# Latent attention: four heads' weighted sums on four column groups together, and an extra product of resident weights ahead of thirteen of sixteen heads' scores

## The reference, cut to what matters

```python
query = qt_c + qt_r            # 16 heads x 256 tokens x 8
key = kt_c + kt_r
value = heads(ct_kv @ Wu_v_w + Wu_v_b)
attn = jnp.einsum('bhqd,bhkd->bhqk', query, key) / scale
attn = jax.nn.softmax(attn, axis=-1)
out = jnp.einsum('bhqk,bhkd->bhqd', attn, value)
out = out.transpose(0, 2, 1, 3).reshape(b, s, d_model)
return out @ Wo_w + Wo_b
```

## Time and profile before

| | |
|---|---|
| median of 3 runs | 2129.3 us (2128.28 to 2129.81) |
| profiled execution, first to last instruction (span) | 2134.5 us |
| latent attention, first scores to last weighted sum | about 1290 to 1788 us of the span |
| TensorE clock, mean granted over the span | 0.890 of full speed |

### The profile page before, as it was taken

One profiled execution on the slowest core, in us unless ns is written; L12 is line 12 of the kernel. 1 busy time (PEld: TensorE's weight loads), 2 busy tenths in 40 slices (PEclk: granted clock), 3 DMA queues, 4 the chain that ended last, 5 costly groups with the idle time before them and its releaser, 6 DMA issues.

```text
span 2134.5 us, 38192 instructions
## 1 busy us (share of the span) xinstructions
PE 1807.3 (85%) x10652; PEld 1360.9 (64%) x10653; DVE 1259.6 (59%) x4249; ACT 688.6 (32%) x1279; POOL 585.9 (27%) x946
## 2 busy tenths in 40 slices
PE   3759993888834599479999979999999998999998
PEld 2548991444433499468888855555555555988997
DVE  2546884666544588656656645655655652656654
ACT  0115550222200255223223214444444443223222
POOL 2653775555247366631221010000000000000000
PEclk9658996787755699789999979999999999999999
DMA  5111212000001122200000000000000000000001
GB/s 196 39 45 50 61 49 92 21 18 19 5 20 43 57 58 60 57 23 11 14 15 10 1 1 1 1 1 0 0 0 0 0 0 1 1 0 0 0 1 40
DMA packets 61674, 54.01 MB, mean 25 GB/s; under 512 B 8467, under 2 KB 54932, under 8 KB 61077
## 3 DMA queue, kind: packets, MB, share of 16 engines
q1 hardware_dynamic: 51958, 34.11, 5.2%
q0 software_dynamic: 8192, 16.79, 2.6%
q10 hardware_dynamic: 1440, 2.10, 0.3%
HBM read 31.48 MB, written 21.50 MB: 25 GB/s over the span
## 4 chain that ended last, share of the span: by engine, by line
PE 70%; issue 10%; DVE 9%; POOL 6%; DMA 2%; SPq 1%; ACT 1%; POOLq 1%; DVEq 1%; ACTq 0%
PE bk L1007 14%; PE bk L1656 10%; PE bk L582 6%; PE bk L990 5%; PE bk L992 5%; PE bk L991 5%; PE bk L1644 3%; PE bk L575 3%; PE bk L1631 2%; PE bk L1582 2%; PE bk L564 2%; PE bk L566 2%; PE bk L565 2%; DMA sb_X<-x 1%; POOL sb_xf L455 1%
## 5 line engine op out<-in xcount | busy, mean ns | idle before, releaser
L1007 PEld LDWEIGHTS bk<-sb_wd,sb_sc 128*128 128x128 f32 (+1 forms) x2688 | 332.9, 191 | 24.8 <-DVE sb_X L1106 3.6
L1007 PE MATMUL bk<-sb_wd,sb_sc 128*128 128x128 f32 (+1 forms) x2688 | 336.9, 275 | 0.9 <-issue 0.8
L1092 DVE TENSOR_TENSOR sb_sc<-sb_sb_,bk 128x512 f32<-128x512 f32 x224 | 152.2, 684 | 240.5 <-PE bk L992 190.4
L112 POOL TENSOR_TENSOR sb_ln_ve<-sb_ln_mv,sb_eps 128x2 f32<-128x2 f32 (+1 forms) x48 | 9.4, 195 | 1010.2 <-DVE sb_ln_mv L104 1010.2
L1046 ACT ACTIVATE sb_sb_<-bk 128x512 f32<-128x512 f32 x224 | 133.9, 598 | 450.8 <-PE bk L992 448.4
L1910 DVE TENSOR_REDUCE sb_sc<-bk 128x2 f32<-128x512 f32 x256 | 164.6, 687 | 156.2 <-PE bk L1631 152.1
L1656 PE MATMUL bk<-sb_sa,sb_sb_ 128*32 128x256 f32 x1024 | 247.4, 385 | 0.7 <-ACT sb_sc L1805 0.7
L1818 ACT ACTIVATE sb_sa<-bk 128x512 f32<-128x512 f32 x256 | 151.1, 597 | 182.8 <-PE bk L1644 182.8
L1106 DVE SCALAR_TENSOR_TENSOR sb_X<-bk,sb_gate,sb_X 128x128 f32 (+1 forms) x576 | 161.4, 342 | 4.2 <-PE bk L1007 1.8
L582 PE MATMUL bk<-sb_w2c,sb_sb_ 128*128 x1152 | 152.1, 275 | 0.0
L368 POOL DMA_INDIRECT xs<-sb_xn,sb_send_row x128 | 128.8, 1006 | 83.6 <-DVE sb_send_row L357 48.3
(11 more groups left out here) (279 smaller groups left out, 3418.7 us busy)
## 6 DMA issues: line engine op xcount, KB each, us to landing
sb_sc<-xs SPq DMA_DIRECT2D x144, 64.0 KB, 1.8
ys<-sb_sc SPq DMA_DIRECT2D x36, 256.0 KB, 2.3
xs<-sb_xn,sb_send_row POOLq DMA_INDIRECT x128
out<-sb_X SPq DMA_DIRECT2D x1, 2048.0 KB, 8.7
sb_sa<-w SPq DMA_DIRECT2D x1, 1792.0 KB, 13.3
sb_sc<-w SPq DMA_DIRECT2D x1, 1792.0 KB, 17.8
sb_sa<-w_gu SPq DMA_DIRECT2D x1, 1760.0 KB
xs<-sb_zeros SPq DMA_DIRECT2D x24, 64.0 KB, 17.8
```

What stands on the lines that cost most here:

```text
L1007: ins = pe.matmul(bank[:, j * P:(j + 1) * P], p.hT[0:m, c % HRING, j * P:(j + 1) * P], p.wd[0:m, q * D:(q + 1) * D], start=(c == FIRST[e] ...
L1092: dve.tensor_tensor(p.hT[0:m, c % HRING, :], p.sg[0:m, c % 2, :], p.bk[2 + c % 2][0:m, :], ALU.mult)\
```

## The change

The weighted sums of four heads are issued together: at steps 5, 9, 13 and 17 instead of one head at each of steps 2 to 17, with the key half as the outer and the head as the inner loop, so that four products in a row have four different column groups. The exponentials therefore stay longer, and their ring grows from four to eight buffers; the four new ones lie in two tensors that this stage did not use (`g2b`, `be2b`). ACT's copy of the first half moves by one head (from after head 9's exponentials to after head 10's). And ahead of the scores of every head but 5, 9 and 13, PE multiplies a resident 128 x 128 weight of the mixture by 512 of its own columns (float32r), into the bank that the scores then overwrite; nothing reads that product.

```diff
--- before.py
+++ after.py
@@ -1535,6 +1535,9 @@
 HQ = P // HR
 NHQ = NH // HQ
 NPROD = 3 * HD
+NQUAD = NH // HQ
+ERING = 8
+WARM_STEPS = [h for h in range(16) if h not in (5, 9, 13)]
 LATENT = 64
 ATT_SCALE = 1.0 / float(np.sqrt(NH + 2 * LATENT))
 SEARCH_BANKS = (1, 2, 5)
@@ -1633,12 +1636,19 @@
     ins.then_inc(p.at_s1.sem, 1)
 
 
+def at_warm_pe(pe, p, bank):
+
+    pe.matmul(bank[:], p.wgh[:, 0:P], p.wgh[:, 0:W], start=True, stop=True)
+
+
 def at_scores_pe(pe, p, b, par, h):
 
     if h % (NH // 2) == 0:
         pe.wait_ge(p.at_q2.sem, p.at_q2.at(2 * b + 2 * h // NH + 1))
     if h >= 2:
         pe.wait_ge(p.at_ex.sem, p.at_ex.at(NH * b + h - 1))
+    if h in WARM_STEPS:
+        at_warm_pe(pe, p, p.bk[3 + h % 2])
     r = head_rows(h, NPROD + 2)
     for t in range(NB2):
         ins = pe.matmul(p.bk[3 + h % 2][:, t * S:(t + 1) * S], p.at_kT[par][r, h // HQ, t * P:(t + 1) * P],
@@ -1646,15 +1656,17 @@
     ins.then_inc(p.at_s2.sem, 1)
 
 
-def at_values_pe(pe, p, b, par, a):
-
-    pe.wait_ge(p.at_ex.sem, p.at_ex.at(NH * b + a + 1))
-    if a % 8 == 0:
-        pe.wait_ge(p.at_op.sem, p.at_op.at(2 * b + a // 8))
-    o = p.bk[7][HR * (a % HQ):HR * (a % HQ + 1), (a // HQ) % 2 * S:((a // HQ) % 2 + 1) * S]
+def at_values_pe(pe, p, b, par, quad):
+
+    pe.wait_ge(p.at_ex.sem, p.at_ex.at(NH * b + HQ * (quad + 1)))
+    if quad % 2 == 0:
+        pe.wait_ge(p.at_op.sem, p.at_op.at(2 * b + quad // 2))
     for t in range(NB2):
-        ins = pe.matmul(o, p.at_v[:, par, t, a, :], p.at_e[:, a % 4, t * S:(t + 1) * S],
-                        start=(t == 0), stop=(t == NB2 - 1))
+        for r in range(HQ):
+            a = HQ * quad + r
+            o = p.bk[7][HR * r:HR * (r + 1), quad % 2 * S:(quad % 2 + 1) * S]
+            ins = pe.matmul(o, p.at_v[:, par, t, a, :], p.at_e[a % ERING][:, t * S:(t + 1) * S],
+                            start=(t == 0), stop=(t == NB2 - 1))
     ins.then_inc(p.at_av.sem, 1)
 
 
@@ -1690,8 +1702,8 @@
     for h in range(NH + LAG):
         if h < NH:
             at_scores_pe(pe, p, b, par, h)
-        if h >= LAG:
-            at_values_pe(pe, p, b, par, h - LAG)
+        if h >= HQ + LAG - 1 and (h - LAG) % HQ == HQ - 1:
+            at_values_pe(pe, p, b, par, (h - LAG) // HQ)
         if h == 1:
             pe.wait_ge(p.at_kr.sem, p.at_kr.at(b + min(ahead, 1) + 1))
             at_maxima_rows_pe(pe, p, b, 1)
@@ -1801,7 +1813,7 @@
 
 def at_heads_out_act(act, p, b, half):
 
-    act.wait_ge(p.at_av.sem, p.at_av.at(NH * b + 8 * half + 8))
+    act.wait_ge(p.at_av.sem, p.at_av.at(NQUAD * b + 2 * half + 2))
     act.activation(flat(p.at_o[:, 2 * half:2 * half + 2, :]), p.bk[7][:], ACT.Copy).then_inc(p.at_op.sem, 1)
 
 
@@ -1813,12 +1825,12 @@
 def at_act_element(act, p, b, par, behind=True, ahead=2):
     for h in range(NH):
         act.wait_ge(p.at_s2.sem, p.at_s2.at(NH * b + h + 1))
-        if h >= 4:
-            act.wait_ge(p.at_av.sem, p.at_av.at(NH * b + h - 3))
-        act.activation(p.at_e[:, h % 4, :], p.bk[3 + h % 2][:], ACT.Exp, scale=ATT_SCALE).then_inc(p.at_ex.sem, 1)
+        if h >= ERING:
+            act.wait_ge(p.at_av.sem, p.at_av.at(NQUAD * b + (h - ERING) // HQ + 1))
+        act.activation(p.at_e[h % ERING], p.bk[3 + h % 2][:], ACT.Exp, scale=ATT_SCALE).then_inc(p.at_ex.sem, 1)
         if h == 1:
             at_maxima_rows_act(act, p, b, 1)
-        if h == 7 + LAG:
+        if h == 8 + LAG:
             at_heads_out_act(act, p, b, 0)
         if ahead >= 1:
             if h == 2:
@@ -2039,7 +2051,7 @@
     "mla": dict(ln_free=B, ln_stat=2 * NT, ln_rs=2 * B, xt=B, at_xc=B, at_ctp=B, at_ct=B, at_krp=B, at_kr=B,
                 at_prp=2 * B, at_q=NS1 * B, at_hc=2 * B, at_ktp=2 * B, at_kt=2 * B, at_qtp=2 * B, at_qt=2 * B,
                 at_s1=NH * B, at_mx=NH * B, at_nm=4 * B, at_q2p=2 * B, at_q2=2 * B, at_s2=NH * B, at_ex=NH * B,
-                at_av=NH * B, at_op=2 * B, at_otp=B, at_on=4 * B, at_tp=B, at_ot=B, at_wp=B, at_x1=B, at_x=B,
+                at_av=NQUAD * B, at_op=2 * B, at_otp=B, at_on=4 * B, at_tp=B, at_ot=B, at_wp=B, at_x1=B, at_x=B,
                 at_init=5),
     "swiglu": dict(_PREP, **_COMB, gt_rows=NCH * NG, up_rows=NCH * NG, silu_d=NCH * NG, hid_d=NCH * NG, exp_d=E1 * NG,
                    exp_add=TG * E1 * NG, rtg=NG, rt3=2 * NG),
@@ -2137,7 +2149,11 @@
     at = Space(t.w1h)
     w.update(at_qT=at.take(P, NHQ, S), at_qT2=at.take(P, NHQ, S))
     at = Space(t.sa)
-    w.update(at_e=at.take(P, 4, NB2 * S), at_sk=at.take(P, 2, NB2, NH, HR))
+    heads = [at.take(P, NB2 * S) for _ in range(4)]
+    w.update(at_sk=at.take(P, 2, NB2, NH, HR))
+    for bank in (Space(t.g2b), Space(t.be2b)):
+        heads += [bank.take(P, NB2 * S) for _ in range(2)]
+    w.update(at_e=heads)
     w.update(at_sk_r=w["at_sk"].bitcast(F32R))
     at = Space(t.sb_)
     w.update(at_v=at.take(P, 2, NB2, NH, HR), at_xa=at.take(P, S), at_c=at.take(P, S), at_r=at.take(P, 2, NB2, D),
```

## The result

The change made the kernel slower: 2224.58 us median (2211.16 to 2230.06, 4 runs) against 2129.56 (2128.28 to 2130.51, 4 runs) of the kernel before, run beside it, a ratio of 1.0438 (95% interval 1.0406 to 1.047). The forecast was 2110 us, with a range of 2068 to 2152. Of the rivals the slower one, C, had the right sign and mechanism, but its time (2148) too was far from the measured one.

What follows compares the result with a forecast made beforehand. PE was taken to pace the latent attention nearly alone. Four legs gave 28.4 against 31.83 us per element, 55 us over 16; low clock took back 2.2 of 3.4 us, leaving 19 us: 2110 us, range 2068 to 2152.

Steps and rivals of the forecast that it cites:

- C: Rival for the attention stage: clock alternates, half the time low, 4.2 low stretches per element, 2148 us; chance 0.20.
- two low stretches per element: Clock term of the attention stage: 1.1 us each, so 2.2 of the 3.4 us gained per element go back.
- two places: Where the clock should fall: while PE waits for DVE's keys, and where only scores, searches and added products stand between groups.
- steps 10 to 12: Between two groups, only scores, searches and added products: one low stretch expected, 1.1 us per element.
- Steps 1 to 3: Element's start, where PE waits for DVE's keys: one low stretch expected, priced at 1.1 us.
- Leg 1: Projection to keys: DVE's twelve instructions end it, four added products fit, unchanged at 6.75 us.
- Leg 2: Keys to queries: 3.65 us at full clock, against 4.28 before.
- Leg 3: Queries to first search: 3.5 us against 4.20, with ACT's copies of the queries late next.
- Leg 4: First search to projection: 14.5 us against 16.60, DVE's reductions fitting under PE's work.
- The group of four: Four heads' weighted sums overlapping on column groups: 1.02 us at full clock, against 0.98 for one head.
- D: Rival: groups overlap only two by two, 1.8 us each, 3.1 us more per element, 2124 us; chance 0.08.
- The added product: Ahead of the scores: 0.31 us each, between 0.23 and 0.43, plus 0.20 where scores used to follow a search directly.

Runs made afterwards that it cites:

- the kernel with two products: The changed kernel with two added products in place of one ahead of each of the thirteen heads: 2123.36 us, ratio 0.9982 to the kernel before.
- the pairs: Against the changed kernel: two heads' sums per group at steps 3, 5, ... 17, ring of four, no added product; 2086.59 us, again 2074.55 us.

## Why the prediction was wrong

**The step that failed** is one sentence of the part on the clock: "I expect two low stretches per element, one at each of the two places". There are 22.3 us of low clock per element, 22.3 / 3.4 = 6.5 of the forecast's stretches. Each cost (37.05 - 28.4) / 6.5 = 1.3 us (37.05 is the mean distance of projections) where 1.1 was taken and up to 1.7 allowed. So 8.65 us per element went back where 2.2 were forecast. Of the 6.45 us between, 4.5 x 1.1 = 5.0 are the number of stretches, the rest their price. 6.45 x 16 = 103 us on 2110 is 2213, beside the 2211.16 us of the profiled run.

Behind it stand two steps. One is the argument against C, that "at half clock the same work fills more of the time, so the clock should rise again sooner". It was false, and rows 6 already spoke against it: 8.3 of 10.3 us busy, the clock at 0.50. Here PE is busy 23.21 of 23.90 us without a rise. The other is the step from rows 7 to "two places". Rows 7 had been read rightly (24-row products do not keep the clock up), but only for steps 10 to 12; the whole way from the first search to the projection had grown thin. In the kernel before, the chain of that leg has 8.6 us of weighted sums in 16.6; here it has 5.7 in 23.3, mostly at half clock, and 3.7 of added products beside 9.0 of scores and searches. Thirteen added products (3 us for the 10 that went) were too few: the clock was 0.69 with them, 0.91 with twice as many. C's threshold (3.1 stretches, a stage clock of about 0.82) fits: of the kernels with groups of four and added products, those at 0.55, 0.69 and 0.80 are slower than the kernel before, those at 0.91 and 0.93 are not.

By places: steps 10 to 12 are low, as forecast. Steps 1 to 3 are not, though PE waits there: from the third element on the clock is 1.00 between projection and keys, as in 1536.60 to 1550.30. PE's longest gap in the stage is 1.2 us, and still the clock was low for 62% of the time; the stretch with the waits (12.04 of 13.70 us busy) is at 1.00, and the next one, busy all 13.70, at 0.50. The Trainium skill (TensorE: Matmul & The Clock Gate, Why this matters for your kernels) asks for no long idle gaps between bursts; this stage had none, so the trace does not agree that this is enough.

**The legs at full clock were right.** Leg 1, 6.75 forecast: 1436.40 to 1443.15 = 6.75 in the kernel with two products. Leg 2, 3.65 forecast: 1542.65 to 1546.19 = 3.54 in the changed kernel. Leg 3, 3.5: 3.34, and ACT's two copies of the queries end it, as said. Leg 4, 14.5: no element of the changed kernel has it at full clock (23.26 us at mostly half); with two products it is 1450.52 to 1466.40 = 15.9, less 0.24 for each of four to six second products (six stand there, four of them in the chain), 14.4 to 14.9. The sum is 28.1 to 28.6 for 28.4. Within that leg 2.4 us of the chain (1456.90 to 1459.26) are DVE's reductions, which the forecast had fitted under PE's work. A misreading without effect on the sum: of the 0.98 us pieces the chain of rows 2 has eleven, not thirteen, and the legs count eleven.

**The group of four** is 1.00 us (forecast 1.02). D is out. The trace has nearly the full four-fold: 3.9 us of single sums in 1.00. The 2.38 that the Trainium skill (TensorE: Matmul & The Clock Gate, Part 3: Packing small matmuls — row/col tiling) gives for three column tiles, scaled to four, would by estimate have made it 1.24.

**The added product**: 0.23 or 0.43, the two bounds, according to what is ahead. Per element 13 x 0.31 + 4 x 0.20 = 4.8 by the forecast's own prices, and 36.57 - 31.83 = 4.7 on the kernel before (36.57 is the median distance of projections with the products in it). The close agreement is partly luck: in leg 1 four products take 1.3 us and lengthen it by 0.9 (7.68 for 6.75). The price was never the trouble. Ring, ACT's moved copy and ACT's wait cost nothing that a run showed: with the clock up, the groups of four run at the forecast's pace.

## What to carry to other kernels

An edit that packs TensorE's work into fewer busy microseconds must be priced twice: by the time saved at full clock, and by what is then left beside the packed pieces, since here a piece of TensorE cost nearly double at half clock (1.00 and 1.9 us). Look in the trace for stretches where the remaining kind of product stands alone; a low granted clock there, with the engine busy, is a warning for the stage to come. Where the clock is at stake, try the smaller step (two heads, not four), and put wide products where the engine waits anyway rather than on the path: that made 2053 us out of 2128, where the larger step lost 95.

## What the runs showed of the hardware

- Four column groups give nearly four-fold throughput: sixteen records of 128 x 32 weights against 256 columns in 1.00 us, of a single head four in 0.98. The order in the program does not matter: head by head or block by block, 1.89 against 1.86 us at half clock.
- The granted clock stays at 0.50 with PE 95 to 100% busy, for up to 23.9 us in a row in the changed kernel, with no gap over 0.7 us in the stretches shown. A product of 128 rows ahead of the scores raised it from 0.59 to 0.69, the same with 32 rows lowered it to 0.55.
- Adding 208 useless products made the changed kernel 100 us faster (2224.6 to 2123.4), and adding 45 where the engine waits made the pairs 21 us faster (2074.6 to 2053.4).
- Work that raises the clock need not profit from it: groups issued twice brought the stage clock from 0.59 to 0.74, and most of them ran at half clock, the two shown in 3.4 us each.
